# Moments taken in the attentions, dense logit products, and a first expert's weights loaded ahead

## The reference

```
x = x + attn0(layernorm(x), ctx)           # 16 heads of 16, each query sees 32 keys
x = x + ffn0(layernorm(x))                 # 16 experts, top 4, and a shared one; width 128
x = x + attn1(ctx, layernorm(x))           # 16 heads of 64; keys: 512 of ctx, 512 of x
x = x + ffn1(layernorm(x))                 # 8 experts, top 2, and a shared one of 2 x 352
layernorm(x) = (x - mean(x)) / sqrt(var(x) + 1e-5)      # over the 256 columns
```

## Time and profile before

| | us |
|---|---|
| median of 3 runs | 3398.57 (3397.33 to 3399.1) |
| profiled execution | 3397.3 |
| its span | 3395.7, mean granted clock 0.954 |
| PE busy | 3141.2 (93%) |
| DVE busy | 2206.5 (65%) |
| POOL busy | 1656.1 (49%) |
| ACT busy | 1342.6 (40%) |

### The profile page before, as it was taken

One profiled execution on the slowest core, in us unless ns is written; L12 is line 12 of the kernel. 1 busy time (PEld: TensorE's weight loads), 2 busy tenths in 40 slices (PEclk: granted clock), 3 DMA queues, 4 the chain that ended last, 5 costly groups with the idle time before them and its releaser, 6 DMA issues. The chain is left out here.

```text
span 3395.7 us, 58842 instructions
## 1 busy us (share of the span) xinstructions
PE 3141.2 (93%) x18285; PEld 2302.8 (68%) x18286; DVE 2206.5 (65%) x5104; ACT 1342.6 (40%) x2058; POOL 1656.1 (49%) x1001
## 2 busy tenths in 40 slices
PE   5885999999879999999999999999999977879978
PEld 4655788888756666666666666666666656679966
DVE  5667455555657777777777777777776663245545
ACT  2332333333334444444444444444444432234422
POOL 5002333333236666666666666666665655770047
PEclk7995999999989999999999999999999977989999
DMA  4000000001111111212121112121211032342253
GB/s 114 1 0 1 20 14 9 14 10 59 78 57 60 66 60 40 78 47 81 38 62 62 63 38 80 45 84 35 66 62 51 11 110 81 131 156 72 72 179 104
DMA packets 118349, 204.62 MB, mean 60 GB/s; under 512 B 13793, under 2 KB 85545, under 8 KB 112433
## 3 DMA queue, kind: packets, MB, share of 16 engines
q1 hardware_dynamic: 105200, 173.30, 15.2%
q0 software_dynamic: 12992, 29.72, 3.0%
HBM read 141.28 MB, written 61.64 MB: 60 GB/s over the span
## 5 line engine op out<-in xcount | busy, mean ns | idle before, releaser
L2281 POOL TENSOR_TENSOR d_acc<-d_acc,d_pr 128x1024 f32<-128x1024 f32 x384 | 936.9, 2440 | 90.8 <-ACT d_pr L2135 60.4
L2135 ACT ACTIVATE d_pr<-d_p 128x1024 f32<-128x1024 f32 x512 | 487.3, 1026 | 239.7 <-PE d_p L2062 239.4
L1995 PE MATMUL d_pO<-d_pr,d_V 128*64 128x512 f32 x2048 | 473.0, 599 | 0.0
L2281 POOL TENSOR_TENSOR d_acc<-d_pr 128x1024 f32<-128x1024 f32 x64 | 153.3, 2395 | 625.1 <-ACT d_pr L2135 625.1
L2191 DVE TENSOR_REDUCE d_nm<-d_p 128x2 f32<-128x1024 f32 x256 | 303.8, 1221 | 87.6 <-PE d_p L2038 87.6
L942 POOL TENSOR_TENSOR e_hs<-e_hf,e_hs 128x512 fp32r<-128x512 f32 x136 | 175.7, 1292 | 365.1 <-ACT e_hs L917 365.1
L2186 DVE CUSTOM_DVE_ANT_0 d_biased<-d_p,d_masked 128x512 f32<-128x512 f32 x512 | 330.5, 688 | 28.1 <-issue 28.1
L1995 PEld LDWEIGHTS d_pO<-d_pr,d_V 128*64 128x64 f32 x2048 | 135.4, 136 | 261.5 <-issue 234.7
L972 DVE SCALAR_TENSOR_TENSOR res<-e_pY,m_Wt,res 128x256 f32<-128x256 f32 x544 | 225.9, 478 | 44.9 <-PE e_pY L878 44.1
L2202 DVE RECIPROCAL d_rb<-d_rb 128x128 f32<-128x128 f32 x256 | 224.6, 920 | 9.3 <-ACT d_rb L2128 9.3
L963 DVE TENSOR_TENSOR e_hf<-e_sl,e_pU 128x512 f32<-128x512 f32 x136 | 93.7, 689 | 209.2 <-ACT e_sl L914 209.2
(11 more groups left out here) (333 smaller groups left out, 5868.2 us busy)
## 6 DMA issues: line engine op xcount, KB each, us to landing
d_W<-w_split SPq DMA_DIRECT2D x30, 1536.0 KB, 6.8
d_masked<-mask_bias SPq DMA_DIRECT2D x64, 256.0 KB
kv_split<-d_parts SPq DMA_DIRECT2D x56, 256.0 KB
d_kv<-kv_split SPq DMA_DIRECT2D x7, 2048.0 KB
x_slots<-m_zeros SPq DMA_DIRECT2D x1, 9088.0 KB
b_x<-x_slots SPq DMA_DIRECT2D x71, 128.0 KB
y_slots<-b_y SPq DMA_DIRECT2D x71, 128.0 KB
xh_split<-m_XH SPq DMA_DIRECT2D x8, 1024.0 KB
```

What stands on the lines that cost most here:

```text
L1995: last = pe.matmul(pO[own[h], :], V[vb][:, s, par * P + h * HD1:par * P + (h + 1) * HD1], pr[:, s % PT, h, :], start=(s == 0), stop=(s == ...
L2135: act.activation(pr[:, n % PT, :, :], slot(st, what, n)[:, :, :], ACT.Exp).then_inc(exp_done, 1)
L2281: pool.tensor_tensor(acc[:, q, :, :], a, pr[:, s % PT, :, :], ALU.add).then_inc(acc_done, 1)
```

## The change

- `res` has a companion `moments` (128 x 32 tiles x 2). Attention 0 fills it: behind each batch's addition DVE takes four `bn_stats`, four `bn_aggr` and copies the results, with a one-column memset behind each wait. Attention 1 fills it with a new unit F, which for four tiles one after the other does `bn_stats`, `bn_aggr` and a copy; it stands in the odd list after r2, but is emitted only in the first step of a batch (for the batch before), and once in the last step, behind YY.
- The routing stages no longer take moments. One addition of epsilon, one root and one reciprocal serve all 32 tiles; then DVE normalises batch by batch. In layer 1 it writes straight to `rows`, and ScalarE's copy goes. PE waits for each tile, not for four.
- The logits are made the other way round: the gate is the loaded operand, the 512 tokens of a batch are moved (two products). DVE copies the 16 x 512 result to SBUF (`take`), and four small products against the identity bring it back to tokens by experts (`spread_out`), one batch later. All loops over batches are written out. Two PSUM banks `pt` are added, which `route1` uses again for its counts.
- The first expert of e0 and of ea gets its raw weights loaded by SP at the head of the routing stage; for ea ScalarE and POOL also split them there, behind their last batch. In e0 the split stays at the head of the experts' block.
- `route0` reuses a buffer, and attention 1 a corner of `acc` for its row of ones.

The core of the diff:

```diff
@@ attention 0, add_results @@
+                        dve.wait_ge(y_added, 2 * b + 2)
+                        dve.memset(r_turn[:, :], 0.0)
+                        for t in range(TPB):
+                            dve.bn_stats(r_st[:, t, :], res[:, bass.ds(b * TPB + t, 1), :].rearrange(
+                                "p a d -> p (a d)")).then_inc(r_stats, 1)
+                        dve.wait_ge(r_stats, TPB * b + TPB)
+                        dve.memset(r_turn[:, :], 0.0)
+                        for t in range(TPB):
+                            dve.bn_aggr(r_mv[:, t, :], r_st[:, t, :]).then_inc(r_moments, 1)
+                        dve.wait_ge(r_moments, TPB * b + TPB)
+                        dve.memset(r_turn[:, :], 0.0)
+                        dve.tensor_copy(io["moments"][:, bass.ds(b * TPB, TPB), :], r_mv[:, :, :]).then_inc(r_kept, 1)
@@ routing stage @@
                 sp.dma_start(gate[:, :, :], io[f"{tag}_gate"]).then_inc(gate_in, 16)
+                first.load(sp)
                 r["sync"](sp)
...
+                def normalise(b, k):
+                    if rows is None and b >= 2:
+                        dve.wait_ge(turned, b - 1)
+                    for t in range(TPB):
+                        tile = b * TPB + t
+                        dve.tensor_scalar(normal(b, k, t), res[:, tile, :], mv[:, tile, 0:1], ve[:, tile:tile + 1],
+                                          ALU.subtract, ALU.mult).then_inc(xhat, 1)
+
+                def take(b, k):
+                    dve.wait_ge(logits_done, b + 1)
+                    if b:
+                        dve.wait_ge(spread, b)
+                    dve.tensor_copy(lt[:, :], pt[k][0:E, :]).then_inc(logits_read, 1)
+
+                dve.tensor_scalar(ve[:, :], mv[:, :, 1], EPS, None, ALU.add).then_inc(var, 1)
+                dve.wait_ge(sd, 1)
+                dve.reciprocal(ve[:, :], ve[:, :]).then_inc(rstd, 1)
+                dve.wait_ge(rstd, 1)
+                for b in range(B + 2):
+                    if b < B:
+                        normalise(b, b % 2)
+                    if b >= 2:
+                        take(b - 2, b % 2)
...
+                def logits(b, k):
                     pe.wait_ge(x_copied, b + 3)
+                    if b >= 2:
+                        pe.wait_ge(logits_read, b - 1)
+                    for c in range(DC):
+                        last = pe.matmul(pt[k][0:E, :], gate[:, c, :], xs[:, k, c, :], start=(c == 0),
+                                         stop=(c == DC - 1))
+                    last.then_inc(logits_done, 1)
+
+                def spread_out(b, k):
+                    pe.wait_ge(logits_read, b + 1)
                     for t in range(TPB):
-                        for c in range(DC):
-                            last = pe.matmul(pl[:, bass.ds(b * TPB + t, 1), :], xs[:, k, c, t * P:(t + 1) * P],
-                                             gate[:, c, :], start=(c == 0), stop=(c == DC - 1))
-                    last.then_inc(logits_done, 1)
+                        last = pe.matmul(pl[:, b * TPB + t, :], lt[:, t * P:(t + 1) * P], ident[0:E, 0:E],
+                                         start=True, stop=True)
+                    last.then_inc(spread, 1)
 
                 turn(0, 0)
-                for_batches(pe, emit)
+                for b in range(B):
+                    if b + 1 < B:
+                        turn(b + 1, (b + 1) % 2)
+                    logits(b, b % 2)
+                    if b:
+                        spread_out(b - 1, (b - 1) % 2)
+                spread_out(B - 1, (B - 1) % 2)
@@ attention 1, DVE, unit F @@
+                            dve.wait_ge(y_added, NSTEP + 1 if last_step else st.g)
+                            dve.memset(turn[:, 2:3], 0.0)
+                            for t in range(TPB):
+                                src = res[:, bass.ds(bb * TPB + t, 1), :].rearrange("p a d -> p (a d)")
+                                dve.bn_stats(xst[:, :], src).then_inc(f_step, 1)
+                                dve.wait_ge(f_step, base + 3 * t + 1)
+                                dve.memset(turn[:, 2:3], 0.0)
+                                dve.bn_aggr(xmv[:, :], xst[:, :]).then_inc(f_step, 1)
+                                dve.wait_ge(f_step, base + 3 * t + 2)
+                                dve.memset(turn[:, 2:3], 0.0)
+                                dve.tensor_copy(io["moments"][:, bass.ds(bb * TPB + t, 1), :].rearrange(
+                                    "p a d -> p (a d)"), xmv[:, :]).then_inc(f_step, 1)
```

More of the change, by code:

```diff
@@ L565, in moe_routes, with normal @@
-        r = route(nc, io, sb, ps, sem, pl, Wt, logits_done, tag)
+        var, sd, rstd, xhat, gate_in, turned, x_copied, hi_done, lo_done, logits_done, logits_read, spread = (
+            sem(f"{tag}_{n}") for n in ("var", "sd", "rstd", "xhat", "gate_in", "turned", "x_copied", "hi_done",
+                                        "lo_done", "logits_done", "logits_read", "spread"))
+        r = route(nc, io, sb, ps, sem, pl, pt, Wt, spread, tag)
+        def normal(b, k, t, c=None):
+            columns = slice(0, D) if c is None else slice(c * P, (c + 1) * P)
+            if rows is not None:
+                return rows[:, bass.ds(b * TPB + t, 1), columns].rearrange("p a d -> p (a d)")
+            return xh[:, k, t, columns]
@@ L596, in _ @@
                         ins.then_inc(lo_done, 1)
+                first.low(pool)
             @block.scalar
@@ L621, in _ @@
                 pe.wait_ge(gate_in, 16)
-                for k in range(2):
-                    pe.matmul(px[k][0:E, 0, 0:E], gate[:, 0, :], gate[:, 0, :], start=True,
-                              stop=True).then_inc(logits_done, 1)
-                pe.wait_ge(logits_done, 2)
                 def turn(b, k):
-                    pe.wait_ge(ls["xhat"], TPB * (b + 1))
                     pe.wait_ge(x_copied, b + 1)
                     for t in range(TPB):
+                        pe.wait_ge(xhat, TPB * b + t + 1)
@@ L631, in turn @@
                         for c in range(DC):
-                            last = pe.transpose(px[k][:, c, t * P:(t + 1) * P],
-                                                xh[:, k, t, c * P:(c + 1) * P], ident[:, :])
+                            last = pe.transpose(px[k][:, c, t * P:(t + 1) * P], normal(b, k, t, c), ident[:, :])
                     last.then_inc(turned, 1)
-                def emit(b, i, k):
-                    if not (isinstance(b, int) and b == B - 1):
-                        turn(b + 1, 1 - k)
+                def logits(b, k):
@@ L781, in moe_experts @@
         sb, ps, sem = scope(nc, ctx)
-        raw_gu = sb(f"{tag}_raw_gu", [P, GU])
-        raw_d = sb(f"{tag}_raw_d", [P, NF, D])
-        Wgu = [sb(f"{tag}_Wgu{k}", [P, 2, GU], F32R) for k in range(2)]
-        Wd = [sb(f"{tag}_Wd{k}", [P, 2, NF, D], F32R) for k in range(2)]
+        loads = first is None
+        first = first or FirstExpert(sb, sem, io, tag, source, skip, F, True)
+        raw_gu, raw_d = first.raw_gu, first.raw_d
+        raw_gu_in, raw_d_in, w_hi, w_lo = first.raw_gu_in, first.raw_d_in, first.w_hi, first.w_lo
+        Wgu, Wd = ([first.Wgu], [first.Wd]) if first.split else ([], [])
+        for k in range(len(Wgu), min(2, NX)):
+            Wgu.append(sb(f"{tag}_Wgu{k}", [P, 2, GU], F32R))
+            Wd.append(sb(f"{tag}_Wd{k}", [P, 2, NF, D], F32R))
         sl = sb(f"{tag}_sl", [P, 2, S])
@@ L904, in split @@
                         act.copy(out[:, HI, :], raw).then_inc(w_hi, 1)
-                split(0, 0)
+                if loads or not first.split:
+                    split(0, 0)
                 def emit(e, j, u, last):
@@ L1046, in layer0_ffn @@
         XH = sb("m0_XH", [P, 2, DC, B * S], F32R)
-        moe_routes(nc, io, res, ident, XH, Wt, "m0", E0, route0)
-        moe_experts(nc, io, res, ident, XH, Wt, "e0", N0, I0, beside=ahead)
+        first = FirstExpert(sb, sem, io, "e0", "e0", 0, I0, False)
+        moe_routes(nc, io, res, ident, XH, Wt, "m0", E0, route0, first)
+        moe_experts(nc, io, res, ident, XH, Wt, "e0", N0, I0, beside=ahead, first=first)
 class Plan:
@@ L1107, in route1 @@
     slot_f = sb(f"{tag}_slot_f", [P, TOPK1, NT])
-    p_counts = [ps(f"{tag}_p_counts{c}", [P, P]) for c in range(KC)]
+    p_counts = [pt[c][:, 0:P] for c in range(KC)]
     p_place = ps(f"{tag}_p_place", [P, TE + E1])
```

168 lines of the change are left out of this document (103 added, 65 removed).

## The result

| | before | changed |
|---|---|---|
| median of 4 runs each, beside one another | 3398.84 us | 3437.76 us (3425.76 to 3440.33) |
| ratio | 1 | 1.011 (95% interval 1.0097 to 1.0123) |
| profiled execution, span | 3397.3, 3395.7 us | 3440.3, 3438.7 us |
| mean granted clock | 0.954 | 0.959 |

A forecast was written before the change was run, and what follows sets the result against it. PE was taken as the path: in attentions added DVE work costs only PE's delay; normalising stages run PE's list at 1.2 GHz. Terms -11.0 - 11.7 - 2.1 - 7.4 + 1.2 + 8.4 + 3.2 = -19.4 gave 3379 us, range 3364 to 3398.

The forecast's parts named there:

- Moments in attention 1: In the loop: 0: Attention 1, unit every eighth step: 3.2 us of DVE work hidden before PE's scores, cost 0, bounds 0 and 22.4.
- if the eighth steps are longer by microseconds: Attention 1: sign that the prediction is wrong; the step with the unit was to be as long as the others.
- A DVE operation from SBUF to SBUF waits while POOL is in one: Normalising stages: a 128x4 TENSOR_SCALAR took 1.21 us beside POOL's two subtractions, 0.17 with POOL idle.
- Rival (b): Attention 1: the unit pushes PE by about its length each time, slack being smaller; +22 gives 3401 us; chance 0.08.
- Routing stages: The two normalising stages: -11.0 us for the first (35.5 against 46.5), -11.7 for the second.
- that the clock rises: Normalising stages: PE's granted clock, 0.53 and 0.50 before, goes near 1.0 from the second batch of each.
- 3.8 us a batch: Normalising stages at 2.4 GHz: taken between PE's 3.5 and 3.87 if POOL's subtractions and DVE's normalising exclude each other.
- POOL's pair: Normalising stages: POOL's two subtractions a batch, 2.49 us; with 1.38 of normalising, at least 3.87 if they exclude each other.
- Attention 0: Moments in attention 0: 6 x 0.8 + 1.5 = 6.3 us in the batches, +2.1 bare at the end, together +8.4.
- passes to PE: Attention 0: of 2.1 us DVE work a batch, 1.34 fills idleness and 0.76 delays PE; 1.5 in the last batch.
- First experts' weights: Head of the experts' blocks: loading ahead gives -2.1 us in layer 0; splitting ahead too gives -7.4 in layer 1.
- the +1.2 that POOL's split was to cost: Layer 1 routing: POOL's split of the shared expert's weights holds back DVE's SBUF operations, between 0 and 4 us.

## Why the prediction was wrong, point by point

- **The step that failed** is "Moments in attention 1: In the loop: 0". It priced the unit at 4 x 0.8 = 3.2 us "from the small operations of the earlier trace rows". Those rows are from a stretch where POOL is idle. The unit was 9.2 us, and in the loop it cost 7 x 6.4 + 6.2 = 51 us in place of 0. The slack was read rightly: the prediction had room for 3.2 + 1.4 = 4.6 us, and 1.8 and 4.35 us at that place cost nothing. The prediction had named this sign itself: "if the eighth steps are longer by microseconds".
- The mechanism was in the prediction's own text, if too wide: "A DVE operation from SBUF to SBUF waits while POOL is in one", 1.21 against 0.17 us. Statistics and aggregates go from SBUF to SBUF too, and aren't held; copies are. I used the sentence for the routing stages and not for the one stage in which POOL is busy 60% of the time. The Trainium skill says which operations are concerned, on the page "SBUF — State Buffer", section "SBUF: two separate sides": those in a 2-port mode or with two SBUF inputs; and the page "VectorE: DVE Perf Modes", section "What auto-detection actually checks", counts a single SBUF source with an SBUF destination among the former, if their outermost dimensions are even or equal. By that the copy is concerned. The traces agree for the copy (1573 against 169 ns).
- Rival (b), 3401 us, had the place and the sign. Its price was the unit's own length, 3.2 a time, and its reason a smaller slack; both were wrong, and the real price twice as high.
- **Routing stages**: that the clock rises was right, and that the old form of the logits had kept it down was shown. 3.8 us a batch was right, its reason wrong: it is PE's list, 3.83 us and not 3.5 (transposes 1.02, dense products 1.82, turning products 0.99, priced at 0.87, 1.7 and 0.9). With POOL's subtractions short it is the same 3.83, so POOL's pair is no bound. Mis-sized: the stages, by 5 and 7 us in this execution and by 1.5 to 9.5 in the others with this code. The start lacks the wait for batch 3 with the clock behind it, 3.4 us; the end lacks a turning product, 1.0 us, and in the second stage the two held operations ahead of the first maximum, some 2 us. I priced the hold as an average over a batch and didn't ask what POOL does when it is first let go.
- **Attention 0**: +10.8 for +8.4, within the bounds. The 0.8 a batch that "passes to PE" was 0.1 to 2.2, and 4.1 in the last batch in place of 1.5, since behind a longer wait of PE's its clock falls.
- **First experts' weights**: -2.2 for -2.1, and -7.8 for -6.2. Right in the ledger, though part of the +1.2 that POOL's split was to cost is booked in the line of the second stage. No run takes these two moves away by themselves.
- With the copy moved to ScalarE the sum comes out at 3377.8. That is partly luck: in that kernel attention 1 is 2.0 us shorter than before and not 3.2 longer, the blocks of routed tokens are 4.1 us shorter for no reason that was forecast, and each stage gives 3.4 us less than forecast.

## What to carry to other kernels

Before an instruction is priced from a row, look at what the neighbours did in that row and what they will do at the new place: a 2-column copy cost 0.16 us beside an idle POOL and 1.7 beside a busy one, an 8-column copy anything from 0.17 to a whole POOL instruction. For copies as small as these the count matters, not the size. Write small results where they are wanted with an operation that isn't held, or let ScalarE move them. And a wait of PE's costs more than its length where the clock falls behind it (4.3 us became 6.4, and 1.6 became 3.4), so the slack of a place is worth reading in the trace before work is put there.

## What the runs showed of the hardware

- Beside a running POOL addition, statistics (0.42 us), aggregates (0.18), memsets (0.06) and reciprocals (0.92 for 128x128, 0.94 beside an idle POOL) on DVE took what they take alone; copies from SBUF to SBUF, a tensor_scalar from SBUF to SBUF (1.43 from one to the next for 0.34, beside subtractions) and operations with two SBUF tensors didn't (the product to `OT` 1136 ns in the changed kernel and 714 with POOL's additions short). ScalarE's copy of the same 8 columns wasn't held (0.21).
- How long an operation is held follows POOL's instruction, not its own size: 1.7 us for 2 columns behind additions of 2.48 us, and 1.43 us for 256 columns behind subtractions of 1.40. A copy that started with POOL's addition or just ahead of it took 0.17 us, one that started 0.01 us behind it 2.37.
- After the same two waits of PE's (0.6 and 0.97 us) the granted clock stayed at 1.00 in two executions of one stage's code and fell in two others: 5.85 and 5.84 us for the batch against 7.30 and 8.63.
